# One core: the order in which half of the softmax exponentials are written, and when the projection weights are split

## The reference

```python
latent_kv = x @ w_kv_down                  # 256 -> 128
k, v = split(latent_kv @ w_kv_up)          # 16 heads of 64 each
q = x @ w_q
att = softmax(where(causal, q @ k.T * 64 ** -0.5, -inf))
x = layernorm(x + (att @ v) @ w_out)
```

## Time and profile before

| what | value |
|---|---|
| median of 3 runs | 3292.0 us (3286.45 to 3294.0) |
| the profiled execution | 3290.01 us, span 3288.2 us |
| PE busy | 2916.1 us, 89% of the span |
| DVE busy | 2307.4 us, 70% |
| ACT busy | 1753.8 us, 53% |
| POOL busy | 1568.3 us, 48% |
| DMA, mean | 196 GB/s, 644.62 MB |
| mean granted TensorE clock | 0.951 |

### The profile page before, as it was taken

One profiled execution on the slowest core, in us unless ns is written; L12 is line 12 of the kernel. 1 busy time (PEld: TensorE's weight loads), 2 busy tenths in 40 slices (PEclk: granted clock), 3 DMA queues, 4 the chain that ended last, 5 costly groups with the idle time before them and its releaser, 6 DMA issues. The chain is left out here.

```text
span 3288.2 us, 53404 instructions
## 1 busy us (share of the span) xinstructions
PE 2916.1 (89%) x17196; PEld 1973.4 (60%) x17196; DVE 2307.4 (70%) x4808; ACT 1753.8 (53%) x3981; POOL 1568.3 (48%) x1661
## 2 busy tenths in 40 slices
PE   7898888888888898888888888869999999999997
PEld 4444444444444444444444444438999999999996
DVE  6777787776778777777687777863697875444546
ACT  5555555555555555555555555544544444444443
POOL 3334334344333433434433343424766777666665
PEclk9999999999999999999998999979999999999998
DMA  4666766676676666667667667677754444443435
GB/s 139 234 230 209 244 230 227 217 252 214 215 245 229 219 223 230 223 218 249 217 216 243 226 215 244 223 253 247 276 177 122 123 102 103 103 103 84 92 67 158
DMA packets 345525, 644.62 MB, mean 196 GB/s; under 512 B 36360, under 2 KB 244616, under 8 KB 337056
## 3 DMA queue, kind: packets, MB, share of 16 engines
q1 hardware_dynamic: 303200, 590.68, 53.0%
q0 software_dynamic: 25152, 33.75, 6.2%
q10 hardware_dynamic: 16896, 16.78, 1.5%
HBM read 347.38 MB, written 293.69 MB: 195 GB/s over the span
## 5 line engine op out<-in xcount | busy, mean ns | idle before, releaser
L214 POOL TENSOR_SCALAR prob<-prob,inv 128x256 f32<-128x256 f32 (+7 forms) x1024 | 748.6, 747 | 1286.4 <-DVE inv L667 1286.4
L524 ACT ACTIVATE prob<-s_ps,neg_max 128x128 f32<-128x128 f32 (+7 forms) x1024 | 755.6, 741 | 770.0 <-DVE neg_max L661 769.2
L661 DVE CUSTOM_DVE_ANT_0 s_ps<-s_ps,mask 128x128 f32<-128x128 f32 (+7 forms) x1024 | 754.7, 772 | 315.9 <-PE s_ps L340 315.6
L675 DVE STREAM_TRANSPOSE squares<-prob 128x640 f32<-128x640 f32 (+3 forms) x512 | 840.8, 1679 | 15.4 <-POOL prob L214 2.2
L386 PE MATMUL o_ps<-late_t,v 128*64 128x512 f32 (+3 forms) x2048 | 415.7, 528 | 22.7 <-DMA late_t<-s_d 20.8
L340 PE MATMUL s_ps<-tok 64*128 64x512 f32 (+3 forms) x1536 | 335.3, 542 | 55.0 <-ACT prob L524 54.1
L340 PE MATMUL s_ps<-k,q 64*128 64x512 f32 (+3 forms) x1536 | 328.3, 532 | 51.3 <-ACT prob L524 50.7
L1679 PE MATMUL e_y<-w_hi,hid_hi 128*128 128x256 f32 (+1 forms) x1088 | 312.1, 287 | 0.0
L1680 PE MATMUL e_y<-w_lo,hid_hi 128*128 128x256 f32 (+1 forms) x1088 | 308.0, 283 | 0.0
L1681 PE MATMUL e_y<-w_hi,hid_lo 128*128 128x256 f32 (+1 forms) x1088 | 308.0, 283 | 0.0
L1540 POOL DMA_INDIRECT acc_d<-yg,idx_all x128 | 211.0, 1649 | 189.7 <-ACT yg L1753 155.7
(11 more groups left out here) (233 smaller groups left out, 5594.1 us busy)
## 6 DMA issues: line engine op xcount, KB each, us to landing
s_d<-squares SPq DMA_DIRECT2D x64, 1024.0 KB, 5.4
late_t<-s_d SPq DMA_DIRECT2D x256, 256.0 KB, 4.3
s_d<-squares SPq DMA_DIRECT2D x64, 896.0 KB, 4.0
late_t<-s_d SPq DMA_DIRECT2D x256, 224.0 KB, 5.2
s_d<-squares SPq DMA_DIRECT2D x64, 768.0 KB, 3.6
late_t<-s_d SPq DMA_DIRECT2D x256, 192.0 KB, 4.5
s_d<-squares SPq DMA_DIRECT2D x64, 640.0 KB, 2.9
late_t<-s_d SPq DMA_DIRECT2D x256, 160.0 KB, 4.3
```

The source lines that it names most:

```text
L214: pool.tensor_scalar(pr, pr, inv[:, i:i + 1], 1.0, ALU.mult, ALU.mult).then_inc(norm_done, 1)
L524: act.activation(prob[i][:, 0:(q + 1) * P], score_part(n, s), ACT.Exp, scale=-1.0, bias=neg_max[:, i:i + 1], accum_out=total[:, i:i + 1]). ...
L661: dve.tensor_tensor_reduce(part, part, mask[:, T - (q + 1) * P:T], 1.0, -MASKED, ALU.add, ALU.min, neg_max[:, i:i + 1]).then_inc(max_done, 1)
L675: dve.transpose(square_all(q).rearrange("p (j h k c) -> p j h k c", j=4, h=2, c=Q)[:, :, h, :, :], prob[(2 * q + h) % PB][:, 0:t * P].rear ...
```

## The change

Three things are changed, all in the attention stage.

The exponentials of slots 4 to 7 are written in another order: `prob` is no longer in key order inside a tile of 128 keys but grouped by key modulo 4. ACT reads the scores in order and writes each element 32 elements (128 bytes) behind the one before, four times, and then goes one element on.

The block transposes of those slots then read 32 neighbouring elements for each block instead of every fourth. What they write is unchanged.

The split of the weights is made for pair n+2 in pair n instead of for pair n+1: ACT does it in slot 5, behind `keep(n + 1, 3)` and ahead of exponential 10, and POOL in slot 4 behind `norm(n, 4)`. Two pairs are split ahead of the loop. SP's program and `load_weights` are not changed.

```diff
@@ gpsimd
-            weights_low(0)
+            for n in range(2):
+                weights_low(n)
...
-                if q == 1 and n + 1 < NPAIRS:
-                    weights_low(n + 1)
+                if q == 4 and n + 2 < NPAIRS:
+                    weights_low(n + 2)
@@ scalar, exp
-                act.activation(prob[i][:, 0:(q + 1) * P], score_part(n, s), ACT.Exp, scale=-1.0,
+                to, made = prob[i][:, 0:(q + 1) * P], score_part(n, s)
+                if q >= 4:
+                    to = to.rearrange("p (k j c) -> p k c j", j=4, c=Q)
+                    made = made.rearrange("p (k c j) -> p k c j", j=4, c=Q)
+                act.activation(to, made, ACT.Exp, scale=-1.0,
                                bias=neg_max[:, i:i + 1], accum_out=total[:, i:i + 1]).then_inc(exp_done, 1)
@@ scalar
-            weights_high(0)
+            for n in range(2):
+                weights_high(n)
...
                     exp(n, 2)
-                    if after:
-                        weights_high(n + 1)
                     exp(n, 3)
...
                 if q == 5:
                     if after:
                         keep(n + 1, 3)
+                    if n + 2 < NPAIRS:
+                        weights_high(n + 2)
                     exp(n, 10)
@@ vector, turn_squares
-                                  prob[(2 * q + h) % PB][:, 0:t * P].rearrange("p (k c j) -> p j k c", j=4, c=Q)
+                                  prob[(2 * q + h) % PB][:, 0:t * P].rearrange("p (k j c) -> p j k c", j=4, c=Q)
```

## The result

| | before | after |
|---|---|---|
| median of 3 runs | 3292.0 us | 3475.06 us (3469.54 to 3475.23) |
| ratio | | 1.0554, 95% interval 1.0529 to 1.058 |
| span of the profiled execution | 3288.2 us | 3473.2 us |
| DVE busy | 2307.4 us | 2008.8 us |
| ACT busy | 1753.8 us | 2067.6 us |

The change makes the kernel 5.5% slower. DVE has 299 us less to do, ACT 314 us more, and neither sum by itself gives the time: ACT stands still for 270 us that did not exist before.

The account below looks back on a forecast made before the run. A ring of handoffs, no full engine, was taken to bound the kernel. A pair: 14.75 + 20.3 + 1.0 for the clock, 36.1 against 33.5 us; +2.6 x 63 = +164 on 3290 gives 3455 us, 3390 to 3520 (overall 3260 to 3640).

Parts of the forecast that it names:

- Faster transposes: DVE's transposes of slots 4 to 7: 1.20, 1.07, 0.95 and 0.82 us for the four widths, 5.3 us less a pair.
- the rival with unchanged transposes: DVE's transposes as slow as before: 35.8 to 37.5 us a pair, 3440 to 3550 us; chance 0.08.
- Slower exponentials: ACT's exponentials of slots 4 to 7, writing with a 128-byte step: 0.94 ns more an element, 6.3 us a pair.
- The rivals with unharmed and twice as slow exponentials: ACT's exponentials unharmed by the step: 3306 us, chance 0.22; twice as much slower: 3675 us, chance 0.13.
- The new wait: ACT ahead of exponential 10 stands still for pair n+2's weights: 4.2 us, 250 to 300 us in all.
- X: Start of exponential 10 on ACT, forecast at T + 14.75 instead of T + 11.5.
- T: End of slot 7's transposes on DVE; the weights were forecast to land at T + 14.2, up to T + 14.8.
- From X to T: From the start of exponential 10 to the next end of slot 7's transposes: 20.3 us, 18.0 with unharmed exponentials.
- The clock: PE's clock falls behind a new 4 us gap ahead of scores 6 and 7: 1.0 us a pair, ends 0 and 1.65.
- Wait for `w_lo` worth nothing: PE's wait for POOL's low weights, 135.6 us in 56 waits, goes; by itself worth about nothing.
- the ring: Chain of handoffs between engines taken to set a pair's time, cut at T and X; 33.0 us at full clock before.
- The rival on the other side, weights in time: Weights land in time and ACT doesn't stand still: 3214 us, or 3070 with unharmed exponentials; chance 0.07.

Follow-up runs that it names:

- the 3351 us kernel: The kernel before with exponentials and transposes unchanged, the weights split late (slot 6) and two pairs split ahead of the loop: 3350.8 us, ratio 1.0188.
- the 3095 us kernel: The kernel before with the new order, exponentials reading PSUM with a step and writing neighbours, split as before: 3095.23 us, ratio 0.9411.
- 3180: The kernel before with exponentials and transposes in the changed order, the split of the weights as before: 3180.15 us, ratio 0.9672.
- 3158: The changed kernel with the split for pair n+2 later, on ACT behind exponential 13 and on POOL behind norm(n, 5): 3158.19 us, ratio 0.9605.
- 3032 us: The changed kernel with the later split, and exponentials that read PSUM with a step and write neighbours: 3032.35 us, ratio 0.9229.

## Why the prediction was right

The forecast was 3455 us (3390 to 3520 for its case), measured 3475. Step by step:

- *Faster transposes.* 1.22, 1.10, 0.97 and 0.85 us against 1.20, 1.07, 0.95 and 0.82. Right; the step in the reads was the price, and the rival with unchanged transposes falls.
- *Slower exponentials.* 2.07, 1.86, 1.57 and 1.41 us for the four widths, against 2.07, 1.85, 1.62 and 1.40 (from 0.90 + 0.72 and the like). The transposes' price for a step, 0.94 ns an element, held for ACT's writes. That the price of one engine's reads at 16 bytes would be that of another's writes at 128 was an analogy, and no run shows why the two agree: the number was in part luck. The rivals with unharmed and twice as slow exponentials fall with these durations.
- *The new wait.* Right in kind and place, 59 waits on the DMA of w_v; in size 269.6 us, inside the stated 250 to 300. The place of X was mis-sized: it is at T + 15.8 in the median, not T + 14.75, and the landing at T + 15.3, beyond even the stated T + 14.8. I had counted on SP writing slot 7's squares 0.2 us behind T as before; with the transposes of slots 6 and 7 closer together SP is still issuing slot 5's reads and the store of y, and writes at T + 1.2 in the median.
- *From X to T.* Predicted 20.3 without the clock; 19.9 to 20.0 measured where the clock stays up (filled gap, later split, earlier load). With fast exponentials 18.0 predicted, 17.9 measured.
- *The clock.* Predicted 1.0 with 1.65 as an end; it was 1.7 (21.7 against 20.0 with the gap filled), at the end and not in the middle.
- *The sum.* 1.0 too little from T to X, 0.7 too little for the clock and 0.3 too much from X to T give 37.5 in place of 36.1; the inner pairs took 37.4. By itself that would be some 80 us more than forecast, above the 3520 stated for this case. The pairs behind a batch end take 31.5, and the mean of all is 37.14: I hadn't seen that the weights are in time there. The seven of them are together some 41 us shorter than at 37.4 each, and the steps over a batch end grew by 3.0 us where the inner ones grew by 3.9. So a part of the first errors was taken back by a second one: that the total came out only 20 us off is partly luck.
- *Wait for `w_lo` worth nothing.* True for the ring at full clock (33.0 us in both), but with the order of before, where the gap only moved, its removal cost 61 us, and these are in the 105 us of the moved split alone too. I had treated that gap as harmless without asking where it would go.

The rival on the other side, weights in time, is what the loads ahead of slot 7's squares show: 3167 us, where I had priced 3214. It was right as a mechanism and wrong as to what SP does.

## What to carry to other kernels

Work that is moved ahead in one queue needs its inputs ahead too: look up when the transfer that feeds it lands, and what that transfer hangs on in its own queue. Here the split went earlier on ACT, its load stayed behind a write that depends on the previous pair, and a faster ring didn't help, because the load is tied to the ring.

A step in an access pattern has to lie somewhere, and its price differs with where it lies and perhaps with how wide it is: 0.79 us in 1024 elements on DVE's reads of SBUF (16 bytes), 0.96 us on ACT's writes to SBUF (128 bytes), nothing on ACT's reads of PSUM (16 bytes). Try the place before trading one engine's time for another's.

Idle time of TensorE isn't free even where nobody waits for it: ask which matmuls come right behind the gap. If they are on the ring, either move the gap or fill it, and leave the matmuls out where there is no gap: here they cost 3 us in each pair that had none.

## What the hardware showed

- ACT, exponential with its sum, 128x1024 fp32: 1114 ns with neighbours on both sides, 1114 ns reading PSUM with a step of 16 bytes, 2069 ns writing SBUF with a step of 128 bytes.
- DVE, 32x32 block transpose of 128x1024 fp32 in SBUF: 2012 ns reading with a step of 16 bytes, 1224 ns reading neighbours.
- TensorE's clock fell to 1.2 GHz in or right behind gaps of 5.2 us (the changed kernel), 3.3 us (the 3351 us kernel) and 2.5 us (the kernel before), and in some pairs even behind 1.96 us (the 3095 us kernel). In the inner pairs of the kernels whose gaps there were at most some 1.8 us long (3180, 3158 and 3032 us) it stayed at 2.4 GHz nearly throughout. 11 idle matmuls a pair, 2.8 us of work for nothing, won 91 us.
